# A conditioned GRU with residual: weights as one transfer each, in another order of features, and other loop bounds on three engines

## The reference, cut to what matters

```python
# x (32, 512, 512), cond (32, 512); all weights (512, 512), biases (512,), all float32
vz, vr, vh = video @ C_z + b_z, video @ C_r + b_r, video @ C + b     # once; video is cond
xz, xr, xh = x @ W_z, x @ W_r, x @ W                                 # for every step
def step(h, xs):                                                     # 512 steps, one after the other
    z = sigmoid(xz_t + h @ U_z + vz)
    r = sigmoid(xr_t + h @ U_r + vr)
    hh = tanh(xh_t + (r * h) @ U + vh)
    h = (1 - z) * h + z * hh
out = x + all h
```

## Time and profile before

| | us |
|---|---|
| median of 3 executions | 2266.47 (2265.84 to 2267.73) |
| the profiled execution's own time | 2264.97 |
| its span in the profile | 2263.1 |
| PE busy | 2185.4 (97%) |
| DVE / ACT / POOL busy | 1754.5 / 1326.6 / 687.8 |
| chain that ended last: PE | 95% |
| granted TensorE clock, mean | 0.997 of full |

### The profile page before, as it was taken

The page is one execution under the profiler, slowest core; times in us unless marked ns, Lnnn a source line. Parts: engine busy times, 40 slices in busy tenths (PEclk is TensorE's granted clock), DMA queues, the critical chain, the costliest instruction groups (busy, mean ns, idle before and its releaser), DMA issues.

```text
span 2263.1 us, 238050 instructions
## 1 busy us (share of the span) xinstructions
PE 2185.4 (97%) x107502; PEld 1797.5 (79%) x107502; DVE 1754.5 (78%) x8226; ACT 1326.6 (59%) x4623; POOL 687.8 (30%) x1546
## 2 busy tenths in 40 slices
PE   2899999999999999999999999999999999999996
PEld 1788878888888887888888888788878888888875
DVE  5687878778778777777777777777777877877874
ACT  3566556566566665666656666556656656656652
POOL 0233333333333333333333333333333333333331
PEclk9999999999999999999999999999999999999998
DMA  9110110110110110111101101101101101101101
GB/s 196 34 38 19 38 38 19 38 37 19 38 33 23 38 35 22 38 29 28 38 24 33 38 24 32 38 19 37 38 19 38 38 19 38 38 20 38 28 11 22
DMA packets 145390, 78.48 MB, mean 35 GB/s; under 512 B 9024, under 2 KB 140608, under 8 KB 145216
## 3 DMA queue, kind: packets, MB, share of 16 engines
q1 hardware_dynamic: 145216, 76.84, 14.1%
HBM read 43.25 MB, written 33.55 MB: 34 GB/s over the span
## 4 chain that ended last, share of the span: by engine, by line
PE 95%; issue 2%; SPq 1%; DMA 1%; DVE 0%; ACT 0%; DVEq 0%; POOLq 0%; POOL 0%
PE p_bank L269 44%; PE c_bank L259 20%; PE banks L297 16%; PE banks L306 15%; SPq L152 1%; DMA x_nat<-in_x_dram 1%; SPq L147 0%; SPq L163 0%; PE p_bank L278 0%; DVE taken L631 0%; DVE state L635 0%; DVE h_t L639 0%; ACT gate_c L430 0%; SPq L155 0%; DVE h_lo L597 0%
## 5 line engine op out<-in xcount | busy, mean ns | idle before, releaser
L269 PE MATMUL p_bank<-w_hi,x_t 128*32 128x384 f16 x16384 | 1183.1, 327 | 2.4 <-issue 1.6
L269 PE MATMUL p_bank<-w_lo,x_t 128*32 128x384 f16 x8192 | 701.7, 327 | 2.2 <-issue 2.2
L269 PEld LDWEIGHTS p_bank<-w_hi,x_t 128*32 128x32 f16 x16384 | 462.3, 97 | 155.2 <-issue 1.5
L259 PEld LDWEIGHTS c_bank<-u,reset_t 128*32 128x32 f32 x32704 | 488.4, 110 | 98.6 <-DVE reset_t L611 71.7
L259 PE MATMUL c_bank<-u,reset_t 128*32 128x64 f32 x32704 | 551.0, 219 | 8.4 <-issue 8.1
L230 POOL TENSOR_TENSOR result<-x_nat,state 128x128 f32<-128x128 f32 x512 | 233.9, 457 | 1010.0 <-DVE h_lo L597 1008.4
L423 ACT ACTIVATE gate_r<-banks,gates_down 128x64 f32<-128x64 f32 x1024 | 265.6, 310 | 359.1 <-PE banks L297 358.1
L430 ACT ACTIVATE gate_c<-c_bank 128x64 f32<-128x64 f32 x1024 | 228.3, 223 | 302.8 <-PE c_bank L259 302.6
L216 POOL TENSOR_TENSOR kept<-keep,state 128x128 f32<-128x128 f32 x512 | 235.7, 460 | 551.3 <-ACT keep L426 551.3
L609 DVE TENSOR_TENSOR reset<-gate_r,state 128x64 f32<-128x64 f32 x1024 | 209.0, 204 | 209.3 <-ACT gate_r L423 205.8
L419 ACT ACTIVATE h_hi<-h_t 128x64 f16<-128x64 f32 x1024 | 261.0, 255 | 148.0 <-DVE h_t L639 80.4
(11 more groups left out here) (68 smaller groups left out, 2749.6 us busy)
## 6 DMA issues: line engine op xcount, KB each, us to landing
x_nat<-in_x_dram SPq DMA_DIRECT2D x256, 128.0 KB, 3.1
out_dram<-result SPq DMA_DIRECT2D x256, 128.0 KB, 2.8
w_stage<-in_L_cond_W_r_dram SPq DMA_DIRECT2D x4, 256.0 KB, 5.4
w_stage<-in_L_cond_W_z_dram SPq DMA_DIRECT2D x4, 256.0 KB, 8.1
w_stage<-in_L_cond_W_dram SPq DMA_DIRECT2D x4, 256.0 KB, 10.8
u<-in_L_cond_U_z_dram SPq DMA_DIRECT2D x4, 256.0 KB, 13.5
u<-in_L_cond_U_r_dram SPq DMA_DIRECT2D x4, 256.0 KB, 16.0
c_w<-in_L_cond_C_r_dram SPq DMA_DIRECT2D x4, 256.0 KB, 12.7
```

The costliest lines, as they stand in the source:

```text
L259: last = nc.tensor.matmul(c_bank[part(j), a, 0:N // HALVES], reset_t[:, part(q)], u[:, C, q, half_cols(j, a)], start=False, stop=q == Q - ...
L269: last = nc.tensor.matmul(p_bank[k][part(j), 0:G * N], x_t[:, c, part(q), a], w[b][:, :, q, cols(j)], start=f == 0, stop=f == GROUPS - 1, ...
```

## The change

The order of features within a group changes: partition (j, s) now holds rows 128 j + 4 s + q of a weight. These are four rows in a row in memory, so a weight is one DMA to 128 partitions with 8 KB for each. State, gates and x parts hold the features of a group in the order (q, s) of this numbering. For that, the columns of the weights are put into that order while they are split (ACT reads them with a step of four elements; DVE makes the low part in four instructions instead of one), U is copied into a new tile `u_c` by ScalarE, cond into `cond_turned` by DVE, x is read with a step of four elements at L386 and L389, and POOL's result reads x and writes the output tile with that step. `base` is put into the order as it is made.

The order of loads becomes W_r, first block of x, W_z, W, cond, U_z, U_r, U, biases, C_r, C_z, C, second block of x; SP then waits for two results before it loads more x. VectorE takes the top of W_r first and makes four of the five low parts after the last scale. The sum of the third set of x moves into step 0.

TensorE's step 1 and its last ten steps are no longer written out: one loop of 128 passes covers steps 1 to 512, so that projections are made in the last two steps and a step 512 that nobody reads is computed. VectorE's loop has 32 steps for each pass, 15 passes, and 32 steps written out. ScalarE's loop and POOL's stay as they were.

```diff
             def load_weights(tile, source, done):
-                rows = source.rearrange("(j q s) e -> j s q e", j=J, q=Q)
-                for p in range(J):
-                    sp.dma_start(tile[part(p)], rows[p]).then_inc(done, 16)
-
+                sp.dma_start(tile.rearrange("p q e -> p (q e)"), source.rearrange("(p q) e -> p (q e)", q=Q)).then_inc(done, 16)
...
+        def in_turn(tile):
+            return tile.rearrange("p (m q s) -> p m q s", q=Q, s=B)
+
+        def by_turn(tile):
+            return tile.rearrange("p (m s q) -> p m q s", q=Q, s=B)
...
-                nc.gpsimd.tensor_tensor(result[o][:, t], x_nat[j % BUFS][:, t], state[:, tt % SLOTS], ALU.add)\
+                nc.gpsimd.tensor_tensor(by_turn(result[o][:, t]), by_turn(x_nat[j % BUFS][:, t]),
+                                        in_turn(state[:, tt % SLOTS]), ALU.add)\
...
-            total_x(TOTAL_STEP % 2, 0, 0, 3)
             pe.wait_ge(x_t_ready, 3)
             project(0, 2, 0, GROUPS)
-            def step(m, tt, last, candidate_in=None):
+            total_x(TOTAL_STEP % 2, 0, 0, 3)
+            pe.wait_ge(s_w_hi, len(SPLITS))
+            pe.wait_ge(s_w_lo, len(SPLITS))
+            pe.wait_ge(s_u_c, 1)
...
-            step(0, 1, True, s_u_in[C])
-            with pe.Fori(0, SETS - 3) as m:
-                for tt in range(2, SET + 2):
-                    step(m, tt, False)
-            for s in range(SET * (SETS - 3) + 2, T):
-                step(s // SET, s % SET, True)
+            with pe.Fori(0, SETS) as m:
+                for tt in range(1, SET + 1):
+                    step(m, tt)
...
             def whole_x(m):
-                nc.scalar.activation(x_whole[m % 2][:], set_of(m), ACT.Copy, scale=x_up[m % 2][:]).then_inc(x_whole_ready, 1)
+                nc.scalar.activation(in_turn(x_whole[m % 2][:]), by_turn(set_of(m)), ACT.Copy, scale=x_up[m % 2][:])\
+                    .then_inc(x_whole_ready, 1)
...
+                for q in range(Q):
+                    last = V.scalar_tensor_tensor(in_turn(low)[:, :, q], whole[:, q], w_up[:, k:k + 1], in_turn(high)[:, :, q],
+                                                  ALU.mult, ALU.subtract)
+                last.then_inc(s_w_lo, 1)
...
-            with nc.Fori(0, PASSES - 1, engines=[dve.engine], hint_back_edge=True) as i:
-                for tt in range(STEPS):
+            with nc.Fori(0, T // ROUND - 1, engines=[dve.engine], hint_back_edge=True) as i:
+                for tt in range(ROUND):
                     step(i, tt, False)
```

More of the change, by code:

```diff
@@ L339, in _, with step @@
             pe.sem_inc(c_mm, HALVES)
-            total_x(TOTAL_STEP % 2, 0, 0, 3)
             pe.wait_ge(x_t_ready, 3)
             project(0, 2, 0, GROUPS)
-            def step(m, tt, last, candidate_in=None):
+            total_x(TOTAL_STEP % 2, 0, 0, 3)
+            pe.wait_ge(s_w_hi, len(SPLITS))
+            pe.wait_ge(s_w_lo, len(SPLITS))
+            pe.wait_ge(s_u_c, 1)
+            def step(m, tt):
                 s = m * SET + tt
                 c, k = tt % SET, tt % 2
[L346 to L352, removed]
+                now = pe.snap(s + 1)
+                halves = [pe.snap(HALVES * s + (a + 1)) for a in range(HALVES)]
                 pe.wait_ge(seeded, now)
@@ L356, in step @@
                 pe.wait_ge(c_seeded, now)
[L357 to L363, removed]
-                candidate_product([(reset_t_ready, a) for a in halves])
[L365 to L369, removed]
-            step(0, 1, True, s_u_in[C])
-            with pe.Fori(0, SETS - 3) as m:
-                for tt in range(2, SET + 2):
-                    step(m, tt, False)
-            for s in range(SET * (SETS - 3) + 2, T):
-                step(s // SET, s % SET, True)
+                if c == TOTAL_STEP:
+                    total_x(TOTAL_STEP % 2, 0, 0, pe.snap(m + (tt // SET + 3)))
+                pe.wait_ge(x_t_ready, pe.snap(s + 3))
+                project(k, (c + 2) % SET, 0, BEFORE_C)
+                candidate_product([(reset_t_ready, a) for a in halves])
+                project(k, (c + 2) % SET, BEFORE_C, GROUPS)
+            with pe.Fori(0, SETS) as m:
+                for tt in range(1, SET + 1):
+                    step(m, tt)
         @block.scalar
@@ L404, in _ @@
                 act.wait_ge(s_w_up, k + 1)
-                nc.scalar.activation(split_of(g, 0), stage_of(g), ACT.Copy, scale=w_up[:, k:k + 1]).then_inc(s_w_hi, 1)
+                high, whole = (t.rearrange("p q e -> p (q e)") for t in (split_of(g, 0), stage_of(g)))
+                nc.scalar.activation(in_turn(high), by_turn(whole), ACT.Copy, scale=w_up[:, k:k + 1]).then_inc(s_w_hi, 1)
+            act.wait_ge(s_u_in[C], 16)
+            nc.scalar.activation(in_turn(u_c.rearrange("p q e -> p (q e)")),
+                                 by_turn(u[:, C].rearrange("p q e -> p (q e)")), ACT.Copy).then_inc(s_u_c, 1)
             nc.scalar.activation(table[:], w_up[:, 0:1], ACT.Sigmoid)
-            act.wait_ge(x_in[1], 16 * J)
-            act.wait_ge(x_summed, 2)
-            sum_x(2, 0)
             act.wait_ge(s_gates_scale, 1)
@@ L439, in step @@
                 now_m = i * (STEPS // SET) + m
+                if first and tt == 0:
+                    act.wait_ge(x_in[1], 16 * J)
+                    act.wait_ge(x_summed, 2)
+                    sum_x(2, 0)
+                if t == SUM_STEP and not more(3):
+                    act.sem_inc(x_summed, 1)
                 if t == SUM_STEP and more(3):
@@ L539, in scales_of_gates @@
                 dve.sem_inc(s_gates_scale, 1)
-            dve.wait_ge(s_cond_in, 16 * J)
-            V.transpose(cond_t[:], cond_nat[:]).then_inc(s_cond_t, 1)
+            top_of_w(R)
             dve.wait_ge(x_totaled, 2)
@@ L554, in _ @@
             scale_of_w(W_C)
+            dve.wait_ge(s_cond_in, 16 * J)
+            link(V.tensor_copy(in_turn(cond_turned[:]), by_turn(cond_nat[:])))
+            V.transpose(cond_t[:], cond_turned[:]).then_inc(s_cond_t, 1)
+            top_of_w(UZ)
             rest_of_w(0)
-            rest_of_w(1)
-            top_of_w(UZ)
-            rest_of_w(2)
             top_of_w(UR)
             scale_of_w(U_GATES)
-            rest_of_w(3)
-            rest_of_w(4)
+            for m in range(1, len(SPLITS)):
+                rest_of_w(m)
             def base_of(g):
                 dve.wait_ge(s_base_mm, g + 1)
-                V.tensor_tensor(base[:, g], base_cell(g), bias[:, g], ALU.add).then_inc(s_base, 1)
+                V.tensor_tensor(in_turn(base[:, g]), by_turn(base_cell(g)), by_turn(bias[:, g]), ALU.add).then_inc(s_base, 1)
             dve.wait_ge(s_bias_in, 16 * J * G)
@@ L592, in more @@
                 def more(sets):
-                    return not (last and m + sets >= STEPS // SET)
+                    return not (last and m + sets >= ROUND // SET)
                 for a in range(HALVES):
@@ L614, in step @@
                     least_x(m % 2, now_m + 2, count)
-                if not (last and tt == STEPS - 1):
+                if not (last and tt == ROUND - 1):
                     if t == SET - 1:
@@ L622, in step @@
                 dve.wait_ge(kept_ready, now)
-                if not (last and tt >= STEPS - TURN_AHEAD):
+                if last and tt >= ROUND - TURN_AHEAD:
+                    dve.sem_inc(x_t_ready, 1)
+                else:
                     ahead_m, c = divmod(tt + TURN_AHEAD, SET)
@@ L646, in step @@
                 turn(1)
-            with nc.Fori(0, PASSES - 1, engines=[dve.engine], hint_back_edge=True) as i:
-                for tt in range(STEPS):
+            with nc.Fori(0, T // ROUND - 1, engines=[dve.engine], hint_back_edge=True) as i:
+                for tt in range(ROUND):
                     step(i, tt, False)
-            for tt in range(STEPS):
-                step(PASSES - 1, tt, True)
+            for tt in range(ROUND):
+                step(T // ROUND - 1, tt, True)
+            dve.sem_inc(seeded, 1)
+            dve.sem_inc(c_seeded, 1)
+            dve.sem_inc(h_lo_ready, HALVES)
+            dve.sem_inc(reset_t_ready, HALVES)
 _INS = ["x", "cond_1024", "L0_cond_W_z", "L0_cond_U_z", "L0_cond_C_z", "L0_cond_b_z", "L0_cond_W_r", "L0_cond_U_r",
```

38 lines of the change are left out of this document (21 added, 17 removed).

## The result

| | before | changed |
|---|---|---|
| median | 2266.15 us | 4070.3 us (4062.33 to 4075.86, 4 runs) |
| ratio | | 1.7957 (1.7921 to 1.7992) |
| span of the profiled run | 2263.1 | 4072.0 |
| PE busy | 2185.4 (97%) | 2706.6 (66%) |
| granted TensorE clock, mean | 0.997 | 0.876 |

The page of the changed kernel: busy time, the chain by engine, and the instruction queues. These answer to the earlier trace rows.

The account below looks back on a forecast made before the run. TensorE, busy 97% of the span, was taken as the bound. 2264.97 - 19.2 - 1.9 - 5 + 13.6 = 2252.5, or 2254 on the median's scale; +597 for lost blocks gave 2851 us, range 2635 to 3130 (all cases kept: 2240 to 3130).

Parts of the forecast that it names:

- the likeliest case: TensorE's loop needs nine instruction blocks and loses one per pass: 127 x 4.7 = +597, 2851 us, chance 0.34.
- the price of the ninth block: Wait per pass of TensorE's loop if only its first block is lost: 4.7 us, between 3.0 and 6.9.
- every block lost: Rival: TensorE refetches all eight blocks each pass, 31.2 us for 16.9, +1820, 4070 us; chance 0.19.
- the 2254: Time on the median's scale if TensorE's loop fits and ScalarE's steps cost nothing; as a rival, chance 0.27.
- VectorE's back edges: VectorE's loop has 14 back edges in place of 6, each extra one 1.7 us: +13.6 us.
- The tail: TensorE's last ten steps, looped instead of written out, take 4.22 us each in place of 61.39 together: -19.2 us.
- The first pass: TensorE's first loop pass holds four steps of 6.1 us and not five: -1.9 us.
- Setup: Loads and weight splits before the first step, with VectorE's chain deciding if loads get faster: -5 us, -6 at best.
- The DVE split in four parts: VectorE's low part of a weight, made in four instructions: same 2048 elements, three extra starts cost nothing.
- C behind U: In the setup, weight C, now loaded after U, lands some 1.9 us later than before: +1 us.
- A rival at +107: TensorE's loop fits, but ScalarE's 16-byte-step reads of x bound two steps in four: 2361 us, chance 0.17.
- the dear end: Upper bound for ScalarE's reads of x with a 16-byte step: one more element time, +0.52 us per instruction.

Follow-up runs that it names:

- e1: Changed kernel with 90 semaphore increments, which nobody waits for, in front of TensorE's loop: 2357.0 us, ratio 1.041 to the kernel before.
- e2: Kernel before the change, with 16 semaphore increments in front of TensorE's loop and nothing else: 3075.55 us.
- e3: Kernel before the change, with 3 semaphore increments in front of TensorE's loop: 2261.4 us.
- e4: Changed kernel with a branch hint on TensorE's loop and no increments: 2344.29 us.
- g3: Kernel before, with TensorE's 128-pass loop and a branch hint on it, VectorE's loop of 64 steps, 40 increments on VectorE: 2241.55 us, ratio 0.9902.
- h1: Kernel before the change, with 16 semaphore increments at the top of VectorE's program and nothing else: 2257.17 us, ratio 0.9969.
- e5: Changed kernel with 90 increments before TensorE's loop, the old feature order, weights loaded in four parts, no 16-byte steps: 2257.61 us, ratio 0.9967.
- f2: Changed kernel with 90 semaphore increments at the top of TensorE's program: 2346.33 us, ratio 1.0357.
- f3: As f2, but ScalarE's x_whole and high part read x with unit step, so the output is wrong: 2247.29 us.

## Why the prediction was wrong

**The mechanism was right, the likeliest case was not.** That TensorE holds eight blocks, that the loop started 90 instructions into one, and that the change makes it need nine: e1, e2, e3 and e4 show this from four sides. The step that failed is the price of the ninth block, "I take 4.7, nearer to the lower end, because VectorE's back edge in the earlier trace rows is a single short wait". That row spoke of how long one wait is, not of how many there are. The runs show nine fetches in each pass, so every block is lost and not one; the pass takes 30.79 us, 31.4 on average, where I had 31.2 for the rival "every block lost", and its 4070 us are the measured time. That it agrees to the microsecond is luck: the 2254 that it builds on had a setup 8 us too good and VectorE's back edges 15 us too dear, and it left out ScalarE's long reads, whose cost in a pass full of fetches no run shows. The rows for it were there, the tail and the first pass with 3.9 us for each block. I discounted them because they need an order of eviction that no row shows. The range then left this case out, with its 0.19.

**The tail.** -19.2; measured -19.1 in g3. Step 512 costs nothing, as said: the last transpose is 5.4 us before the end of the span in g3 (2238.4 - 2233.01), 5.3 before.

**The first pass.** -1.9; five steps took 30.49 us before, 29.05 in g3, -1.4, and 30.7 in e4, no gain.

**VectorE's back edges.** +13.6; measured -1: fourteen of 0.65 for six of 1.7. I took it that each costs the same. Where the loop lies sets 1.0 of the 1.65 us (h1), by chance in the change's favour, as it was to its harm on TensorE.

**Setup.** -5; measured +3.1 to +3.5 (first state at 57.19 us in e4 and 57.52 in the changed kernel, 54.06 before). The loads did get faster, and more than I had dared to use: 352 to 383 GB/s for 220. The Trainium skill's rule of ports (SBUF — State Buffer, Door 1) agrees with this. The rows of a transfer grew from 2 to 8 KB as well, and no run separates the two. As I said, VectorE's chain then decides; the term that I mis-sized in it is "The DVE split in four parts moves the same 2048 elements and I cost the extra three starts at nothing". The low parts of W_z and W on VectorE and TensorE's first projections, which wait for them, in the changed kernel and then in e5, which has the four parts but no 16-byte steps:

```profile
33.17 8.29 DVE L541 SCALAR_TENSOR_TENSOR w_lo<-w_stage,w_up,w_hi 128x512 f16<-128x512 f32 x8
...
41.72 0.51 PE L280 MATMUL p_bank<-w_hi,x_t 128*32 128x384 f16 x4 [9.43 <-DVE w_lo L541]
```

```profile
33.21 5.39 DVE L546 SCALAR_TENSOR_TENSOR w_lo<-w_stage,w_up,w_hi 128x512 f16<-128x512 f32 x8
...
38.86 0.51 PE L283 MATMUL p_bank<-w_hi,x_t 128*32 128x384 f16 x4 [6.52 <-DVE w_lo L546]
```

The three low parts of W_r, W_z and W take 12.5 us, 8.1 in e5 and 7.0 before. So the extra starts cost 1.1 us and VectorE's reads with a step of 16 bytes 4.4, which eats what the loads gave: the first projection begins at 41.72 us for 38.18 before, and the chain to the first state runs over it. ScalarE's splits doubled too, from 2.00 to 3.92 us each, but VectorE goes from 33.17 to the end of its low parts at 50.3 without a wait for them. One more reading was wrong: C behind U lands later by a whole weight, 4.8 us at the 220 GB/s of the old loads, and not by 1.9. In e5, which has those loads, C's product starts at 50.77 us for 47.04; in the changed kernel, with the fast loads, nothing waits for C.

**ScalarE's reads.** A rival at +107, with the dear end of one more element time. Measured +99 (f2 - f3), with 1276 ns for 713 and 1278 for 877 in e4. With the loop in place, the changed kernel takes 2344 to 2346 us; the rival said 2361, with a setup 8 us too good and back edges 15 us too dear. The Trainium skill's rule that 16-byte lines want two hits each (SBUF — State Buffer, Specifications (TRN2)) agrees in that the new reads are dearer. By how much differs: 512 elements took 0.56 us more in x_whole, 1.1 ns for each, and 0.40 us more in the high part, and POOL's 128 elements took 0.07 us more.

**How the sum comes out.** 2265.0 - 19.1 (tail) + 3.1 (setup) - 1.1 (back edges) + 99 (ScalarE) = 2346.9, for 2344.3 in e4. The pass itself is read from the transposes that end steps 4 and 508, 126 passes apart, in the changed kernel and then in e4:

```profile
83.25 0.24 DVE L653 STREAM_TRANSPOSE h_t<-state 128x64 f32<-128x64 f32 x1
...
4037.72 0.24 DVE L653 STREAM_TRANSPOSE h_t<-state 128x64 f32<-128x64 f32 x1
```

```profile
83.55 0.24 DVE L653 STREAM_TRANSPOSE h_t<-state 128x64 f32<-128x64 f32 x1
...
2324.46 0.24 DVE L653 STREAM_TRANSPOSE h_t<-state 128x64 f32<-128x64 f32 x1
```

That is 31.38 us a pass for 17.79; 127 times the 13.6 us between them are 1727, and 2344 + 1727 = 4071.

## What to carry to other kernels

On an engine whose loop just fits, the code in front of the loop is part of its cost: count the instructions from the engine's start, see in how many blocks the loop lies, and look at the packets of its instruction queue in the middle of the run, where there should be none. A branch hint on the loop is one line; here it took off 1726 us and made harmless a position that needs nine blocks without it. Before a load is made faster by a new order of data, price the new order wherever it is read: a step of 16 bytes added 4.4 us to the three splits of VectorE that TensorE waits for in the setup and held up 256 steps of the run.

## What was not expected of the hardware

A loop that runs over by a little cost half of one that runs over by more: with 11 instructions in its eighth block by the count one pass in two was bad (3075.55 us), with 88 all were (4070.3). An empty semaphore increment on TensorE takes 0.15 us (13.75 us for 90), so it is a poor filler. The hint of e4 needs none. VectorE pays for a step of 16 bytes as ScalarE does: two low parts of 2048 elements took 8.29 us for 5.39 in e5. And the same displacement of a loop that ruins one engine helps another: 16 instructions took 1.0 us off each of VectorE's back edges.
